# A gated feed-forward and a generated adapter on one core: a generator one step later, more banks for tile 1, and up weights in eight loads

## The reference, cut to what matters

```python
# x: (32, 256, 256), cond: (32, 64); up_w: (2048, 256), down_w: (256, 1024)
scale = cond @ norm_w.T + 1.0
h = x * (scale[:, None, :] * rsqrt(mean(x * x, -1) + 1e-6))
val, gate = split(h @ up_w.T, 2, axis=-1)
h = val * gelu(gate)
x = act_quant(h) @ weight_quant(down_w).T + x          # 8 bit by row; ternary by mean |down_w|
dWd = ((cond @ Wdd.T + bdd) * 0.1).reshape(32, 128, 256)   # one adapter per sequence
dWu = ((cond @ Wdu.T + bdu) * 0.1).reshape(32, 256, 128)
down = relu(einsum('bld,bnd->bln', x, Wd + dWd) + bd)
out = x + einsum('bln,bdn->bld', down, Wu + dWu) + bu
```

## Time and profile before

| | us |
|---|---|
| median of 3 runs | 480.67 (480.03 to 480.86) |
| the profiled execution | 480.89 |
| its span, first to last instruction | 479.2 |
| TensorE busy | 467.1 (97%) |
| VectorE / ScalarE / GpSimd busy | 377.8 (79%) / 365.5 (76%) / 260.2 (54%) |
| mean granted TensorE clock | 0.995 of 2.4 GHz |

### The profile page before, as it was taken

One profiled execution on the slowest core, in us unless ns is written; L12 is line 12 of the kernel. 1 busy time (PEld: TensorE's weight loads), 2 busy tenths in 40 slices (PEclk: granted clock), 3 DMA queues, 4 the chain that ended last, 5 costly groups with the idle time before them and its releaser, 6 DMA issues.

```text
span 479.2 us, 10039 instructions
## 1 busy us (share of the span) xinstructions
PE 467.1 (97%) x3278; PEld 271.3 (57%) x3278; DVE 377.8 (79%) x789; ACT 365.5 (76%) x636; POOL 260.2 (54%) x676
## 2 busy tenths in 40 slices
PE   8989999999999999999999999999999999999995
PEld 7445656666565455555555555555555555555563
DVE  4798988898898787877877788786777877777776
ACT  5889999999997678768676876867776777777662
POOL 0295775657655446475573746557374543444653
PEclk9999999999999999999999999999999999999997
DMA  7957787777873455565554466455445544544332
GB/s 269 349 113 205 180 244 227 189 210 181 253 176 89 92 121 100 137 147 117 148 133 107 128 141 155 111 153 126 103 136 133 143 103 119 130 123 90 72 85 89
DMA packets 117860, 71.01 MB, mean 148 GB/s; under 512 B 102000, under 2 KB 102960, under 8 KB 115632
## 3 DMA queue, kind: packets, MB, share of 16 engines
q1 hardware_dynamic: 117648, 70.29, 57.2%
q10 hardware_dynamic: 160, 0.07, 0.1%
HBM read 37.44 MB, written 8.39 MB: 96 GB/s over the span
## 4 chain that ended last, share of the span: by engine, by line
PE 88%; DVE 5%; ACT 3%; issue 2%; DMA 1%; POOL 0%; DVEq 0%; ACTq 0%; SPq 0%; POOLq 0%
PE bank L1022 64%; PE bank L1036 11%; PE bank L1113 4%; PE bank L1127 4%; PE bank L1095 4%; PE bank L993 1%; DVE adapt L716 1%; ACT gel L552 1%; DVE xs_lo L746 1%; DMA qT<-qn 1%; DVE hid L767 1%; DVE amax L775 1%; ACT tern L650 0%; ACT qn L574 0%; DVE x L879 0%
## 5 line engine op out<-in xcount | busy, mean ns | idle before, releaser
L767 DVE SCALAR_TENSOR_TENSOR hid<-bank,rms,gel 128x512 f32<-128x512 f32 x127 | 95.2, 750 | 80.4 <-ACT gel L552 79.4
L552 ACT ACTIVATE gel<-bank,rms 128x512 f32<-128x512 f32 x127 | 86.9, 684 | 90.7 <-PE bank L1022 90.6
L1022 PE MATMUL bank<-up_hi,xs_hi 128*128 128x512 f16 x508 | 151.2, 379 | 3.0 <-DVE hid L767 1.5
L1022 PE MATMUL bank<-up_lo,xs_hi 128*128 128x512 f16 x508 | 151.1, 379 | 0.7 <-DVE up_lo L931 0.7
L1022 PE MATMUL bank<-up_hi,xs_lo 128*128 128x512 f16 x508 | 151.1, 379 | 0.0
L1022 PEld LDWEIGHTS bank<-up_lo,xs_hi 128*128 128x128 f16 x508 | 49.6, 98 | 60.9 <-DVE up_lo L931 1.4
L1022 PEld LDWEIGHTS bank<-up_hi,xs_lo 128*128 128x128 f16 x508 | 49.7, 98 | 59.9
L775 DVE TENSOR_REDUCE amax<-hid 128x1 f32<-128x1024 f32 x63 | 76.9, 1220 | 2.2
L565 ACT ACTIVATE hid<-hid,amax 128x1024 f32<-128x1024 f32 x64 | 72.4, 1132 | 2.3 <-DVE amax L781 1.8
L403 POOL TENSOR_TENSOR wsplit<-stage,wsplit 128x288 f16<-128x288 f32 x64 | 52.8, 853 | 34.9 <-ACT wsplit L527 34.9
L1022 PEld LDWEIGHTS bank<-up_hi,xs_hi 128*128 128x128 f16 x508 | 48.3, 98 | 38.5 <-DVE xs_lo L746 2.9
(11 more groups left out here) (129 smaller groups left out, 633.3 us busy)
## 6 DMA issues: line engine op xcount, KB each, us to landing
xT_s<-in_xT SPq DMA_DIRECT2D x32, 256.0 KB, 3.0
xn_s<-in_xn SPq DMA_DIRECT2D x32, 256.0 KB, 3.1
stage<-in_WddT SPq DMA_DIRECT2D x8, 1024.0 KB, 5.4
stage<-in_WduT SPq DMA_DIRECT2D x8, 1024.0 KB, 5.2
out<-out_s SPq DMA_DIRECT2D x31, 256.0 KB, 2.4
adapt<-in_up_wT SPq DMA_DIRECT2D x4, 512.0 KB, 6.8
x<-in_down_wT SPq DMA_DIRECT2D x1, 1024.0 KB, 10.0
qT<-qn SPq DMA_TRANSPOSE x63, 3.1
```

The costliest lines, as they stand in the source:

```text
L552: nc.scalar.activation(gel[:, c], u_gate[c][:], ACT.Gelu, scale=rms[:, t // TPB % XN_SLOTS, t % TPB:t % TPB + 1]).then_inc(gelu_done, 1)
L767: nc.vector.scalar_tensor_tensor(out=hid[:, t % 2, c * 512:(c + 1) * 512], in0=u_val[c][:], scalar=rms[:, t // TPB % XN_SLOTS, t % TPB:t % ...
L1022: ins = nc.tensor.matmul(dst[:], a[:, t // TPB % 2, k, cols], w[:, c, k, v, :], start=(k == 0 and n == 0), stop=(k == KD - 1 and n == 2))
```

## The change

- The generator is a step later: chunk(s, lag) and adapter_step add one; scales(s) leaves sequence 2 to step 3 instead of 2.
- Tile 1 gets banks of its own (5, 6, 7, 4), so it doesn't wait for tile 0; tile 2 takes the banks of tile 0. down(0) and down(1) go to step 4, residual(0) to step 4, residual(1) and (2) to step 5; from then on as before.
- The up weights come in eight pieces of 256 KB, each with its own semaphore, and are split into high and low parts piece by piece. xn of sequence 0 and 1 comes behind them, the down weights in two halves, the small weights before the first chunk. On ScalarE both squares come behind the copies, on VectorE the root of sequence 0 behind up_lo.
- The absolute sum is in two halves with two matmuls, in step 2; the three ternary passes are all in step 2, behind gate(2,0), gate(2,1) and quant_scale(2). Seven keep-warm matmuls instead of nine in the second group.
- At the end: q is transposed ahead of down(62), middle(30) ahead of the transposes of x of tile 62 and the low part of 63; total(28), residual_high(61) and the output bias of sequence 30 come earlier, and the last output biases wait for VectorE's residual_low.

The core of the diff (most lines of context and the renamings are left out):

```diff
--- before.py
+++ after.py
@@ -64,12 +64,13 @@
 OUT_SLOTS = 3
-N_SMALL = 6
+N_BASE = 4
+N_SMALL = 2
 IDLE_FIRST = 8
-IDLE_SECOND = 9
+IDLE_SECOND = 7
@@ -83,7 +84,7 @@
 def adapter_step(b):
-    return max(2 * b + 7, NGEN + 5 + (4 * b + 2) // 3)
+    return max(2 * b + 7, NGEN + 6 + (4 * b + 2) // 3)
@@ -96,12 +97,23 @@
 def scales(s):
-    return [b for b in range(1, B) if max(2 * b - 2, 1) == s]
+    return [b for b in range(2, B) if max(2 * b - 2, 3) == s]
+def downs(s, c):
+    late = {(4, 0): [0], (4, 1): [1]}
+    return late.get((s, c), [s - DOWN] if c == 0 and s - DOWN >= 2 else [])
+def residuals(s):
+    return {4: [0], 5: [1, 2]}.get(s, [s - DOWN] if s - DOWN > 2 else [])
 def chunk(s, lag):
-    return [s - 2 - lag] if 0 <= s - 2 - lag < NGEN else []
+    return [s - 3 - lag] if 0 <= s - 3 - lag < NGEN else []
 def sequences(s, lead):
...
@@ -197,7 +209,10 @@
         out_ps = [bank[5], bank[6]]
-        sum_ps = y_ps[:, 0:1]
+        sum_ps = bank[5][:, 0:1]
+        second_val = [bank[5], bank[7]]
+        second_gate = [bank[6], bank[4]]
...
@@ -351,16 +371,22 @@
             sp.dma_start(cond2[0:C, :], condT).then_inc(ld_cond, 16)
-            load_x(0)
-            for n in range(NC * KD):
-                sp.dma_start(raw_up[:, n // KD, n % KD], up_wT[:, n // KD, n % KD]).then_inc(ld_up[n], 16)
-            load_x(1)
-            sp.dma_start(raw_down, down_wT).then_inc(ld_down, 16)
+            sp.dma_start(xT_s[:, 0], xT[0]).then_inc(ld_xT[0], 16)
+            up_pieces = up_wT.rearrange("p c k (v f) -> p (c k v) f", v=2)
+            for n in range(NC * KD * 2):
+                sp.dma_start(raw_up[:, n], up_pieces[:, n]).then_inc(ld_up[n], 16)
+            for b in range(2):
+                sp.dma_start(xn_s[:, b], xn[b]).then_inc(ld_xn[b], 16)
+            for i in range(2):
+                part = slice(i * JF * D // 2, (i + 1) * JF * D // 2)
+                sp.dma_start(raw_down[:, part], down_wT[:, part]).then_inc(ld_down[i], 16)
+                if i == 0:
+                    sp.dma_start(xT_s[:, 1], xT[1]).then_inc(ld_xT[1], 16)
+            for i, (w, b) in enumerate(((WdT, bddT), (WuT, bduT))):
+                sp.dma_start(base[:, i, :], w).then_inc(ld_base, 16)
+                sp.dma_start(bias_raw[:, i, :], b).then_inc(ld_base, 16)
+            load_x(2)
             load_chunk(0)
-            load_x(2)
-            for i, (w, b) in enumerate(((WdT, bddT), (WuT, bduT))):
-                sp.dma_start(base[:, i, :], w).then_inc(ld_small, 16)
-                sp.dma_start(bias_raw[:, i, :], b).then_inc(ld_small, 16)
@@ -452,11 +478,10 @@
-            def output_bias_last():
-                for i in LAST_ORDER:
-                    pool.wait_ge(x1_done, LAST_T + i)
-                    nc.gpsimd.tensor_tensor(late_out[:, i], x1[:, (LAST_T - 1 + i) % X1_SLOTS], bu_row[:], ALU.add
-                                            ).then_inc(outb_done, 1)
+            def output_bias_last(i):
+                pool.wait_ge(x1_done, LAST_T + i)
+                nc.gpsimd.tensor_tensor(late_out[:, i], x1[:, (LAST_T - 1 + i) % X1_SLOTS], bu_row[:], ALU.add
+                                        ).then_inc(outb_done, 1)
             def output_bias(b):
...
@@ -494,8 +519,7 @@
                     low_part(q)
                 for b in scales(s):
-                    if b > 1:
-                        rsqrt(b)
+                    rsqrt(b)
@@ -508,10 +532,13 @@
             residual_low(LAST_T - 2)
+            output_bias(B - 2)
             middle_low(B - 3)
-            output_bias(B - 2)
+            pool.wait_ge(x1_lo_done, LAST_T - 2)
+            output_bias_last(1)
             middle_low(B - 2)
-            output_bias_last()
+            output_bias_last(0)
         def _(act):
...
@@ -632,23 +659,30 @@
+            def absolute_sum(i):
+                part = slice(i * JF * D // 2, (i + 1) * JF * D // 2)
+                act.wait_ge(ld_down[i], 16)
+                nc.scalar.activation(tern[:].rearrange("p j d -> p (j d)")[:, part], raw_down[:, part], ACT.Abs,
+                                     accum_out=wsum[:, 3 * i:3 * i + 1]).then_inc(absum_ready, 1)
             scaled_high(0)
+            for n in range(NC * KD * 2):
+                act.wait_ge(ld_up[n], 16)
+                nc.scalar.activation(up_part(up_hi, n), raw_up[:, n], ACT.Copy, scale=U_SCALE
+                                     ).then_inc(up_hi_ready, 1)
             squares(0)
-            for n in range(NC * KD):
-                act.wait_ge(ld_up[n], 16)
-                nc.scalar.activation(up_part(up_hi, n // KD, n % KD), raw_up[:, n // KD, n % KD], ACT.Copy, scale=U_SCALE
-                                     ).then_inc(up_hi_ready, 1)
+            squares(1)
+            absolute_sum(0)
             for s in range(NT):
                 if s == 0:
+                    gelu(0, 1)
                     scaled_high(1)
-                    squares(1)
-                    gelu(0, 1)
-                    act.wait_ge(ld_down, 16)
-                    nc.scalar.activation(tern[:].rearrange("p j d -> p (j d)"), raw_down, ACT.Abs,
-                                         accum_out=wsum[:, 0:1]).then_inc(absum_ready, 1)
+                if s == 1:
+                    absolute_sum(1)
+                    gelu(1, 1)
@@ -658,22 +692,21 @@
                     quantized(s - 1)
-                if 0 < s < LAST_T:
+                if 1 < s < LAST_T:
                 for b in scales(s + 1):
-                    if b > 1:
-                        squares(b)
+                    squares(b)
             quantized(LAST_T)
+            residual_high(LAST_T - 2)
             qT_evacuate()
-            residual_high(LAST_T - 2)
...
@@ -923,26 +956,22 @@
             scaled_low(0)
+            for n in range(NC * KD * 2):
+                dve.wait_ge(up_hi_ready, n + 1)
+                nc.vector.scalar_tensor_tensor(out=up_part(up_lo, n), in0=raw_up[:, n], scalar=U_SCALE,
+                                               in1=up_part(up_hi, n), op0=ALU.mult, op1=ALU.subtract
+                                               ).then_inc(up_ready, 1)
             rsqrt_first()
-            for n in range(NC * KD):
-                c, k = n // KD, n % KD
-                dve.wait_ge(up_hi_ready, n + 1)
-                nc.vector.scalar_tensor_tensor(out=up_part(up_lo, c, k), in0=raw_up[:, c, k], scalar=U_SCALE,
-                                               in1=up_part(up_hi, c, k), op0=ALU.mult, op1=ALU.subtract
-                                               ).then_inc(up_ready, 1)
+            rsqrt_guess(1)
             for s in range(NT):
                 gate(s, 0)
-                if s == 0:
-                    scaled_low(1)
-                    rsqrt_guess(1)
                 if s == 2:
-                    ternary_second()
-                    ternary_third()
-                if s >= DOWN:
-                    residual(s - DOWN)
+                    ternary_first()
+                for t in residuals(s):
+                    residual(t)
@@ -952,15 +981,18 @@
                 for b in scales(s):
-                    if b > 1:
-                        rsqrt_guess(b)
+                    rsqrt_guess(b)
                     gate(s, 1)
+                    if s == 0:
+                        scaled_low(1)
+                    if s == 2:
+                        ternary_second()
                     quant_scale(s)
-                    if s == 1:
-                        ternary_first()
+                    if s == 2:
+                        ternary_third()
@@ -972,6 +1004,7 @@
             residual(LAST_T - 2)
+            total(B - 4)
@@ -980,7 +1013,6 @@
             x62_evacuate()
-            total(B - 4)
@@ -1006,19 +1038,21 @@
             def up(t, c):
-                after(pe, gelu_done, (t - 1) * NC + c + 1)
-                after(pe, hid_done, (t - 1) * NC + c + 1)
+                held = 0 if t == 2 else t - 1
+                if t != 1:
+                    after(pe, gelu_done, held * NC + c + 1)
+                    after(pe, hid_done, held * NC + c + 1)
                             pe.wait_ge(xs_done, t // TPB + 1)
-                        if t == 0 and n == 0:
-                            pe.wait_ge(up_hi_ready, c * KD + k + 1)
-                        if t == 0 and n == 2:
-                            pe.wait_ge(up_ready, c * KD + k + 1)
-                        for v, dst in enumerate((u_val[c], u_gate[c])):
+                        for v, dst in enumerate(u_banks(t, c)):
+                            if t == 0 and n == 0:
+                                pe.wait_ge(up_hi_ready, (c * KD + k) * 2 + v + 1)
+                            if t == 0 and n == 2:
+                                pe.wait_ge(up_ready, (c * KD + k) * 2 + v + 1)
@@ -1160,17 +1194,21 @@
                 up(s, 0)
-                if s >= DOWN:
-                    down(s - DOWN)
+                if s == 2:
+                    pe.wait_ge(hid_done, NC + 1)
```

(14 more changed lines are left out.)

19 lines of the change are left out of this document (11 added, 8 removed).

## The result

The changed kernel takes 484.01 us (median of 5, 483.25 to 484.43), the kernel before, run beside it, 480.67 us (median of 5, 480.03 to 482.0). The ratio is 1.0068, 95% interval 1.0052 to 1.0083: 0.7% slower. 484.5 was predicted, with a range of 480.8 to 487.8. The profiled execution took 483.25 us, the lowest of the five, and its span is 481.5 us; before it was 479.2. So the trace shows a loss of 2.3 us where the medians show 3.3. In the first experiment one of seven executions took 490.82 us at a mean granted clock of 0.949; it is disturbed, and it is left out of that experiment's median.

The account below looks back on a forecast made before the run. TensorE, busy 97% of the span, was taken as the bound. Terms 3.8 + 2.3 - 1.1 - 3.2 + 2.0 = +3.8 us on 479.2 gave a span of 483.0, a median of 484.5; range 480.8 to 487.8.

Parts of the forecast that it names:

- The late root: Step 4: sequence 2's root, behind low_part(0) on GpSimd, ready at 42.4 us; gelu(4,0) and down(1) wait; +3.8 us.
- Rival 1: Start: GpSimd ends the root of sequence 2 by 37.1 us, in time for gelu(4,0); 479.0 us; chance 0.09.
- Step 5: down(2) waits on TensorE for residual(1), which follows gate(5,0) on VectorE; +2.3 us idle, 2.2 to 2.9.
- Near 157 us: TensorE's wait for xs_lo after the last generate goes, evacuations falling on even step 20; -1.1 us.
- The clock in the start: Granted clock halves after TensorE idles; none to two falls of 1.7 us; +2.0 us, bounds 0 and +3.4.
- low clock ahead of up(4,0): First idle stretch, 3.3 us before up(4,0): costs nothing, since TensorE has 5 us of slack before down(1).
- The end: Last steps: residual_low without bias beside it, earlier q transposes, middle(30) in idle time; -3.2 us, range -3.7 to -1.5.
- The pieces: Up weights in eight half pieces: earlier first matmul gives nothing; a rival had slower landing, up to +0.8 us, 485.3.
- The total: Whole kernel: terms sum to +3.8 us on the span, 483.0; 484.5 as a median, range 481.4 to 487.6.
- the chain's 3.8: Loss at step 5: up(5,0) starts at 46.7 us plus 1.4 for a generate, against 44.3; +2.0 to +5.3.

Follow-up runs that it names:

- the first experiment: Changed kernel with GpSimd making the root of sequence 2 before its half of generator chunk 0 in step 3: 478.42 us, ratio 0.9943 to the kernel before.
- the kernel kept warm: Two kernels: in the start, changed kernel plus eleven keep-warm matmuls before down(1), 482.65 us; at the end, kernel before plus three such matmuls, 480.48 us.

## Why the prediction was right, and where it was not

**The late root.** Right, and it carries the result. The chain ran 0.7 to 0.8 us ahead of the one laid out by hand from quant_scale(2) on: 29.60 for 30.3, high_part(0) 32.35 for 33.0, GpSimd 35.46 for 36.2, root 41.69 for 42.4, gelu 41.72 for 42.5, down(1) 43.73 for 44.45. All of that offset arises between the first gate and quant_scale(2), because up to there the trace is 0.4 late (first gate 16.62 for 16.2; the last copy ended at 12.55, not 12.2). From the first gate to quant_scale(2) 14.1 us were laid out (the terms as printed add to 14.2) and 13.0 passed. The term most mis-sized is that of the ternary passes. They were priced from passes that took 1.37 and 1.63 us and took 1.28 and 1.22 in the changed kernel, with their small ones some 2.8 us instead of 3.3. Gates and maxima, which overlap their neighbours a little, took some 0.4 and 0.2 us less; the wait for gelu was 0.58, as laid out (0.5). Rival 1 priced a root in time at 479.0 us; the kernel with the root ahead of the chunk gave 478.42, in its profile with one fall of the clock, as priced. The price was right, and so was the reason for giving it 0.09: the root was 4.6 us too late, not one.

**Step 5.** Right: 2.11 us for 2.3 in the trace, and 1.9 from the edit that removes it.

**Near 157 us.** Right: the wait is in the kernel with only the new end and gone in every kernel with the later generator. The later generator was not run by itself.

**The clock in the start.** Right in kind, one fall behind the wait of 5.3 us. "A little more than one" fall, 2.0 us, was too much for the profiled execution: it was one, 1.5 us by the trace and 1.4 by the kernel kept warm. The idle time of 2.11 us in step 5 brought no fall. The Trainium skill, TensorE: Matmul & The Clock Gate, Part 1, has the half rate as the state to which an idle TensorE returns; the rows at 44 us agree. That low clock ahead of up(4,0) would cost nothing, because TensorE has slack before down(1), was right, though the wait there was 1.75 us and not 3.3. The changed kernel's profile has no fall there, but those of the kernels with the old biases and with four pieces do, 0.50 at 34 to 36 us, and in both down(1) then waited 3.6 us instead of 5.3: the slack took up the 1.7 us. In the kernels with the root in time that slack is gone, and the prediction did not ask what the fall would cost there.

How long TensorE stood idle does not settle whether the clock falls. The 2.11 us in step 5 brought no fall in six traces; 1.97 to 2.38 us ahead of up(4,0) brought one in five traces and none in two. Three of the five executions of the changed kernel had a mean clock of 0.992 or 0.993 against 0.995 in the profiled one, so the profile may show less low clock than the median holds.

**The end.** -3.2 was predicted and -3.7 measured, and this is where the reasoning was weaker than its total. I had put 1.2 us of it to the clock, since 3.4 us of slow matmuls must have cost that much. The trace of before held the counter-evidence: of the slow matmuls only the six of `middle` are in the chain, while behind the twelve stands a wait of 0.40 us for GpSimd's mid_lo, which grows when they are faster. The kernel kept warm shows 0.6 us in its trace. What I had left to the new order, 2.4 us at the low clock and with the bias in it, is 3.1 us by subtraction.

**The pieces.** Right in being near nothing. The chain's start was set by how the loads landed, which differs between executions by more than any effect of their size.

**The total.** The terms add to +3.8, the medians of the five runs to +3.3, the profiled spans to +2.3. Against the trace it was too high by 0.7 in the chain (3.8 for 4.6 - 1.5), 0.2 in step 5, 0.5 in the clock and 0.5 at the end, and too low by 0.4 for small changes between step 6 and the last pieces, which it didn't have: 1.5 in all. The medians fit better, because the profiled execution was the fastest of its five; part of the closeness of 484.5 to 484.01 is luck. The medians of the experiments give a sum of their own: the new end alone 477.86, then 5.6 for the root with its clock fall, 1.9 for step 5 and -1.1 near 157 us make 484.3. One sum of the prediction is off: with bounds of 0.5, 0.3 and 1.1 us the chain's 3.8 has the range 1.9 to 5.7, not 2.0 to 5.3. The 3.1 us measured lie within either.

**What stays open.** How much `middle(30)` alone is worth, where the low clock lay in the executions without a profile, and what the own banks of tile 1 and the new order of down(0) and down(1) are worth, which no kernel changed by themselves.

## What to carry to other kernels

When work moves a step later, write down what stands beside it in each queue that it enters: a chain of twelve tiny instructions stood behind 3 us of bulk work before too, and was 2.5 us ahead of its reader. When the bulk moved a step later it took the chain along, and the reader waited 5.5 us; putting the chain first cost a few lines. A reader that needs its producer in the same step of another engine (`down(2)` behind `residual(1)`) cost 2.1 us in each of the six traces that kept it. And before crediting faster matmuls, look whether they are in the chain that ends last. Those that are not, with a wait for another engine behind them, only make that wait longer.
